# B products on GpSimd at the head of a tile, and the residual through an identity matmul, in a two-layer Mamba and MoE kernel

## What is computed

```python
def mamba_block(seq, ...):
    u, z = split(in_proj(seq)); u = silu(causal_conv4(u) + conv_b)
    dt, Bm, Cm = split(u @ x_proj_w.T)
    dt = softplus(dt @ dt_proj_w.T + dt_proj_b)
    def step(h, inputs):                      # 128 channels d, 16 states n
        dA = exp(dt_t[:, :, None] * A)
        h = dA * h + (dt_t * u_t)[:, :, None] * B_t[:, None, :]
        y = einsum('bdn,bn->bd', h, C_t)
    y = (ys + u * D) * silu(z)
    return y @ out_proj_w.T
...
x = x + mamba(ln(x));  t = tokens(x);  t = t + experts(ln(t))      # twice
```

## Time and profile before

| what | us |
|---|---|
| median of 3 runs | 1973.01 |
| lowest and highest run | 1966.05, 1973.41 |
| the profiled execution's own time | 1973.6 |
| its span | 1971.8 |
| PE busy | 1445.4 (73%) |
| DVE busy | 1359.6 (69%) |
| POOL busy | 1138.6 (58%) |
| ACT busy | 928.1 (47%) |

### The profile page before, as it was taken

One profiled execution on the slowest core, in us unless ns is written; L12 is line 12 of the kernel. 1 busy time (PEld: TensorE's weight loads), 2 busy tenths in 40 slices (PEclk: granted clock), 3 DMA queues, 4 the chain that ended last, 5 costly groups with the idle time before them and its releaser, 6 DMA issues. The chain is left out here.

```text
span 1971.8 us, 28551 instructions
## 1 busy us (share of the span) xinstructions
PE 1445.4 (73%) x7776; PEld 980.9 (50%) x7777; DVE 1359.6 (69%) x1913; ACT 928.1 (47%) x1695; POOL 1138.6 (58%) x788
## 2 busy tenths in 40 slices
PE   6666766667656599999956766666667662799993
PEld 4333333333314499999834333333333222799992
DVE  2899999999995422222143999999999967444443
ACT  6666677667743011111136666677666731011111
POOL 0687788888880244444302888888878850355540
PEclk9889898998968699999968788998998866899996
DMA  3655566555638110111034565566555634111114
GB/s 110 147 135 121 129 144 146 125 126 134 145 79 354 54 41 32 38 37 36 26 126 98 129 138 121 129 143 139 134 121 135 148 136 188 38 48 48 47 41 152
DMA packets 75964, 217.61 MB, mean 110 GB/s; under 512 B 11856, under 2 KB 27408, under 8 KB 72592
## 3 DMA queue, kind: packets, MB, share of 16 engines
q1 hardware_dynamic: 67664, 194.53, 38.9%
q0 software_dynamic: 8256, 22.56, 3.5%
HBM read 178.34 MB, written 38.70 MB: 110 GB/s over the span
## 5 line engine op out<-in xcount | busy, mean ns | idle before, releaser
L669 POOL TENSOR_TENSOR L_hc<-L_h,L_cbq 128x1536 f32<-128x1536 f32 x192 | 660.1, 3438 | 210.6 <-DVE L_h L587 207.5
L492 ACT ACTIVATE ps<-L_dwq,L_negA 128x384 f32<-128x384 f32 x768 | 426.7, 574 | 227.4 <-DVE L_h L587 215.5
L364 PE MATMUL ps<-L_hc,same 128*32 128x384 f32 x1536 | 190.0, 571 | 238.9 <-POOL L_hc L669 238.9
L574 DVE TENSOR_TENSOR L_dbu<-L_dwq,ps 128x768 f32<-128x768 f32 x288 | 270.7, 941 | 29.4 <-DVE L_carry L649 13.1
L587 DVE TENSOR_TENSOR_SCAN L_h<-ps,L_h,L_dbu 128x384 f32<-128x384 f32 x288 | 275.0, 1002 | 12.9 <-ACT ps L492 12.8
L587 DVE TENSOR_TENSOR_SCAN L_h<-ps,L_carry,L_dbu 128x384 f32<-128x384 f32 x288 | 274.2, 1001 | 6.5 <-DVE L_dbu L574 4.7
L364 PEld LDWEIGHTS ps<-L_hc,same 128*32 128x32 f32 x1536 | 31.5, 113 | 358.2 <-POOL L_hc L669 324.3
L1151 DVE COPY Xn<-L_w 128x2048 f32 x86 | 107.6, 1253 | 117.1 <-PE ps L1101 108.3
L1134 ACT ACTIVATE L0e_hT<-ps 128x512 f32<-128x512 f32 x86 | 51.3, 597 | 267.2 <-PE ps L1101 267.2
L678 POOL TENSOR_TENSOR L_dbp<-L_dwq,L_cbq 128x768 f32<-128x768 f32 x96 | 175.1, 1824 | 0.0
L323 PE MATMUL ps<-Xn,L_fold 128*128 (+1 forms) x480 | 103.3, 368 | 89.2 <-DVE L_dw L595 89.2
(11 more groups left out here) (278 smaller groups left out, 2301.4 us busy)
## 6 DMA issues: line engine op xcount, KB each, us to landing
L_dwq<-dw_rows SPq DMA_DIRECT2D x192, 384.0 KB, 6.2
L_cbq<-cb_rows SPq DMA_DIRECT2D x192, 240.0 KB, 9.9
dw_rows<-L_dw SPq DMA_DIRECT2D x48, 384.0 KB, 2.3
L_w<-in_up SPq DMA_DIRECT2D x16, 1024.0 KB, 11.7
L_w<-in_down SPq DMA_DIRECT2D x8, 1024.0 KB, 26.6
tok_rows<-Xn SPq DMA_DIRECT2D x6, 768.0 KB, 13.1
L0s_got<-results SPq DMA_DIRECT2D x18, 256.0 KB, 2.9
L1s_got<-results SPq DMA_DIRECT2D x18, 256.0 KB, 3.5
```

The lines of the kernel that those rows point to most:

```text
L364: mm = nc.tensor.matmul(y_ps[g * QW:(g + 1) * QW, :], same[:, 0:QW], hc[:, (k % 2) * Q + g, :], start=False, stop=(k == Q - 1))
L492: nc.scalar.activation(da(r, c), dwq[:, r, c % Q, 0, :], ACT.Exp, scale=negA[:, 0, c:c + 1]).then_inc(sem["da"], 1)
L574: nc.vector.tensor_tensor(dbu[:, at:at + 2, :], dwq[:, r, 2 * i:2 * i + 2, 1, :], spread(b_ps(r, k)), ALU.mult).then_inc(sem["dbu"], 1)
L669: nc.gpsimd.tensor_tensor(hc[:, at:at + Q, :], h[:, Q * k:Q * k + Q, :], cbq[:, r, k, :].unsqueeze(1).to_broadcast([P, Q, T]), ALU.mult).t ...
```

## The change

Four of the 16 B products of a tile were made by POOL, two behind C0 and two behind C1. Now six are: scans 10 and 11 take theirs from `times_b2` (two planes), scans 12 to 15 from `times_b3` (four planes in one instruction), and both stand ahead of C0 in POOL's order. DVE makes five products of two planes instead of six, and `dbu` has ten planes of its own instead of a ring of six. B of the third quarter is sent through DRAM with the rest, so that `cbq` and `bc` have six rows instead of five (each `cbq` load is 288 KB). The residual is no longer added by DVE: PE adds X to the output's PSUM bank by a matmul with the identity, and ACT copies the sum back to X behind decay 14 (`take_x`).

```diff
-QR = Q + 1
+QR = Q + 2
...
-        dbu = sb("dbu", [P, 6, T])
-        dbp = sb("dbp", [P, Q, T])
+        dbu = sb("dbu", [P, 10, T])
+        dbp = sb("dbp", [P, 6, T])
...
             def spread_b(t, r, k):
-                wait(pe, sem["dbu"], 6 * t + 2 * k - 2)
+                wait(pe, sem["dbu"], 5 * t + (-1, 0, 2)[k])
...
             def project_out(t):
                 pe.wait_ge(sem["yz"], t + 1)
+                x = X[:, :, bass.ds(t * PT, PT)].rearrange("p i (h w) -> p h i w", w=SIDE)
+                nc.tensor.matmul(zb_ps[:, 0:T // 2].rearrange("p (h i w) -> p h i w", i=2, w=SIDE), ident[:], x,
+                                 start=True, stop=False)
                 for j in range(2):
                     mm = nc.tensor.matmul(zb_ps[:, 0:T // 2], w_out[:, j, :], js(yz[:])[:, j, :],
-                                          start=(j == 0), stop=(j == 1))
+                                          start=False, stop=(j == 1))
...
+            def take_x(t):
+                act.wait_ge(sem["out"], t + 1)
+                x = X[:, :, bass.ds(t * PT, PT)].rearrange("p i (h w) -> p h i w", w=SIDE)
+                nc.scalar.copy(x, zb_ps[:, 0:T // 2].rearrange("p (h i w) -> p h i w", i=2, w=SIDE)).then_inc(sem["res"], 1)
...
+                    if c == 14 and not (isinstance(t, int) and t == 0):
+                        take_x(t - 1)
...
-                    if k < Q - 1:
+                    if 2 * k + i < 5:
                         times_b(t, r, p, k, i)
...
-                        if j == 6:
-                            residual(t - 1)
...
+            def times_b2(t, r, p):
+                pool.wait_ge(s_cb[r], 64 * (p + 1))
+                pool.wait_ge(s_dw[r], 64 * (p + 1))
+                wait(pool, sem["scan"], (t - 1) * N + 12)
+                nc.gpsimd.tensor_tensor(dbp[:, 0:2, :], dwq[:, r, 2:4, 1, :], spread(cbq[:, r, Q + 1, :]), ALU.mult
+                                        ).then_inc(sem["dbu_p"], 1)
+
+            def times_b3(t, r):
+                wait(pool, sem["scan"], t * N)
+                nc.gpsimd.tensor_tensor(dbp[:, 2:6, :], dwq[:, r, :, 1, :],
+                                        cbq[:, r, Q, :].unsqueeze(1).to_broadcast([P, Q, T]), ALU.mult
+                                        ).then_inc(sem["dbu_p"], 1)
...
             def tile(t, r, p, last):
+                times_b2(t, r, p)
+                times_b3(t, r)
                 for k in range(Q):
                     times_c(t, r, p, k)
-                    if k < 2:
-                        times_b(t, r, p, k)
                     if k == 2 and not last:
                         lost(t + 2)
```

More of the change, by code:

```diff
@@ L559, in _ @@
             tile_pairs(act, pair)
+            take_x(NT - 1)
         @block.vector
@@ L567, in times_b @@
                     dve.wait_ge(s_dw[r], 64 * (p + 1))
[L568 to L573, removed]
+                at = 4 * k + 2 * i
+                wait(dve, sem["scan"], (t - 1) * N + at + 2)
                 nc.vector.tensor_tensor(dbu[:, at:at + 2, :], dwq[:, r, 2 * i:2 * i + 2, 1, :], spread(b_ps(r, k)),
@@ L577, in scan @@
             def scan(t, c, slot):
-                k, g = c // Q, c % Q
+                k = c // Q
                 dve.wait_ge(sem["da"], t * N + c + 1)
-                if k < Q - 1:
-                    dve.wait_ge(sem["dbu"], 6 * t + c // 2 + 1)
+                if c < 10:
+                    dve.wait_ge(sem["dbu"], 5 * t + c // 2 + 1)
                 else:
-                    dve.wait_ge(sem["dbu_p"], 2 * t + g // 2 + 1)
+                    dve.wait_ge(sem["dbu_p"], 2 * t + (1 if c < 12 else 2))
                 wait(dve, sem["hc"], Q * (t - 1) + k + 1)
@@ L587, in scan @@
                 nc.vector.tensor_tensor_scan(h[:, c, :], da(t % 2 if isinstance(t, int) else int(slot is None), c),
-                                             dbu[:, c % 6, :] if k < Q - 1 else dbp[:, g, :], first, ALU.mult, ALU.add
+                                             dbu[:, c, :] if c < 10 else dbp[:, c - 10, :], first, ALU.mult, ALU.add
                                              ).then_inc(sem["scan"], 1)
@@ L602, in gate @@
                 nc.vector.tensor_tensor(yz[:], zs[:, r, :], y_ps, ALU.mult).then_inc(sem["yz"], 1)
[L604 to L608, removed]
             nc.vector.tensor_tensor(fold[:].rearrange("p g d -> p (g d)"), par("in_u"), par("taps"), ALU.mult
@@ L653, in _ @@
             gate(NT - 1, 1)
-            residual(NT - 1)
         @block.gpsimd
@@ L724, in send @@
                 bc_out, dt_out, w = count(t + 1), count(t + 1), count(t + 1)
-                decayed, driven, mixed, driven_p = count((t - 1) * N), count((t - 1) * 6), count((t - 1) * Q), count((t - 1) * 2)
+                decayed, driven, mixed, driven_p = count((t - 1) * N), count((t - 1) * 5), count((t - 1) * Q), count((t - 1) * 2)
                 sp_.wait_ge(sem["bc_out"], bc_out)
@@ L1370, in pack @@
     state = g("x_proj_w")[4:].reshape(2, Q, Q, P)
-    put("bc", np.concatenate([state[1].transpose(1, 0, 2), state[0, Q - 1][:, None]], 1).reshape(Q * QR, P).T)
+    put("bc", np.concatenate([state[1].transpose(1, 0, 2), state[0, Q - 1][:, None], state[0, Q - 2][:, None]], 1).reshape(Q * QR, P).T)
     put("brep", np.repeat(state[0].reshape(N, P), QW, 0).T)
```

## The result

The changed kernel takes 2027.57 us (median of 4, 2027.01 to 2044.25) against 1973.2 before: ratio 1.0305, 95% interval 1.0276 to 1.0335. It is slower by 3%. The profiled execution took 2027.01, with a span of 2025.0.

A forecast was written before the change was run, and what follows sets the result against it. It took the bound to be the loop from POOL's C3 through C0, PE, ACT and scans: 22.2 + 0.94 = 23.14 us a tile against 22.17, so 1973.6 + 46.6 + 4 = 2024, rounded to 2025; range 1976 to 2060.

The forecast's parts named there:

- No gain from DVE's B product ahead of scan 8: DVE before scan 8: ACT's decay 8 sets the scan, so removing the product is worth 0 to 0.26 us, taken as 0.
- The residual's 0.45 a tile: DVE behind scan 13: without the residual the next B product could begin at 321.33 instead of 321.78, worth 0.45 us.
- Its replacement hidden: Residual through PE (0.4 to 0.8 us more) and ACT's copy (0.45 us at most), covered by other waits: worth 0.
- a sign of being wrong: C3 to C3 above 22.2 for another reason: the two `cbq` users, `lost`, or `take_x` in front of decay 15.
- C0 at 8.5, the loop of 22.2: POOL's C0 starts 8.5 us after C3, 3.2 later; through y0, `project_dt`, Abs and scans, C3 to C3 takes 22.2.
- The loop against the undisturbed tile: C3 to C3 at full clock: 22.2 us against 21.60 and 22.55, mean 22.08, so +0.1 a tile.
- The clock, 0.94 a tile: PE's low clock moves to y0 in five tiles of eight, 1.5 us each: 0.94 a tile, ends 0 and 2.2.
- in more than half of the tiles: Sign of being right: PE's granted clock is low from y0 on in more than half of the tiles.
- The start of a layer, 4 us in both: B products before the first C0 of a layer cost 0 to 5.2 us, taken as 2 for each layer.
- The late `cbq`: Rival: the larger load lands late and delays POOL's chain, costing from 2.4 us of lateness on; 0.10 together with every tile paying.
- DVE's busy time: Sign of being right: DVE's busy time falls by 48 x 1.27 = 61 us and the span doesn't follow.
- the loop without the clock: Rival: POOL's loop holds but PE's clock adds nothing, 22.2 to 22.5 us a tile, 1979 to 1993; chance 0.20.

## Why the prediction was right

It said 2025 with 1976 to 2060, and 2027.57 was measured. The chain, the waits and the loop are as predicted. How the added time parts into loop and clock is not, and that the sum came within 3 us owes something to luck. One more row of the trace before is needed, the C3 that follows those of the earlier trace rows:

```profile
413.98 3.43 POOL L669 TENSOR_TENSOR L_hc<-L_h,L_cbq 128x1536 f32<-128x1536 f32 x1
```

Point by point:

- *No gain from DVE's B product ahead of scan 8.* Right. Scan 8 waits for ACT's decay 8 either way, and the wait grows by what the product took (28.7 against 3.8 us in a stage; 26.1 in 23 tiles is 1.13 each, and 1.15 was predicted). The totals agree twice (1963.75 against 1962.14; stages 1033.1 against 1033.8).
- *The residual's 0.45 a tile.* Too large as its price. It was read from a tile in which the residual itself was late; the typical tiles give 0.21 to 0.26. The loop of 22.2 doesn't suffer from it, since it starts from the same tile and takes the lateness away with the residual.
- *Its replacement hidden.* Right by itself: no loss with it alone. ACT's copy takes 0.30, the identity matmul 0.59 at the full clock. In the changed kernel it is not fully hidden, since the copy waits for `project_out` and decay 15 stands behind it; the prediction named this as a sign of being wrong and gave it no price. Its stages are 3.8 us longer with the replacement than without.
- *C0 at 8.5, the loop of 22.2.* Right: 8.57, and 22.23 and 22.11 when the clock is up. The Abs wait of 1.0 and 0.1 is 0.9 and 0.04 there. That this loop runs over `project_dt` behind y0 is shown by the move of `project_dt` and `project_bc` (1976.8).
- *The loop against the undisturbed tile.* Here the prediction had +0.1 us, against 22.08. Both tiles of the earlier trace rows were a little disturbed. The tile that follows them took 21.39 (392.59 to 413.98), and 21.39 and 22.42 are the usual lengths, with PE kept busy too (21.40 and 22.42). Their mean is 21.91, so the loop is 0.27 a tile longer. In the stages it is more: with PE kept busy in both kernels they are 1064.9 and 1044.5, a difference of 20.4 us or 0.43 a tile. Of it 9.8 us lie in the first four tiles of the two layers.
- *The clock, 0.94 a tile.* The sum set 22.2 + 0.94 against a mean of 22.17 that had the old kernel's clock losses in it. So it counted 0.03 a tile for the loop and 0.94 for the clock. The runs give 0.43 for the loop with the layers' starts and 0.65 for the clock (1.07 in the changed kernel less 0.43 in the one before). The two errors point opposite ways: 46.6 predicted for the stages, 51.5 measured. The picture behind the 0.94 was partly wrong as well. It was not five tiles of eight with two instructions slow. In the first layer it was every second tile, from the fourth on, with all three slow (Abs waits 2.96), in the second two tiles in all; so the sign "in more than half of the tiles" did not come true. The rest of the loss came where a low stretch on `u_in` holds up DVE's product. The prediction had named `u_in` only as a place where low stretches do no harm.
- *The start of a layer, 4 us in both.* The first tile, from scan 0 to scan 0, grew by 0.8 and 3.1 us.
- *The late `cbq`.* Didn't happen beyond the first tile.
- *DVE's busy time.* It fell by 49 us and not by 61. The 61 adds up lengths of instructions, and neighbours overlap: the product of 0.93 in the earlier trace rows held up the next scan by some 0.87.

The rival "the loop without the clock" gave 1979 to 1993. The changed kernel with PE kept busy runs at 1972.7, 6 us under that range. So that rival nearly describes this kernel once the clock is held up.

Open: the parts outside of the Mamba stages are 906 to 915 us in these runs, without an edit there, and I don't know why.

## What to carry to other kernels

An engine that is 96% busy need not be worth relieving: read at each place which wait would be next. Here DVE already waited 0.26 us for ACT. When work is moved ahead of an old instruction, follow that instruction's consumer and everything that is queued behind the consumer on its own engine; here the edit was on POOL and the harmful wait on DVE, by way of PE and ACT. And a wait of PE can cost twice, if it brings the low clock onto the path: keep PE's gaps off the critical queue, or fill all of them.

## What the runs showed of the hardware

- A late operand can cost more by the clock than by its lateness. In the changed kernel ACT's Abs waited 2.96 us for `project_dt` where PE ran at the low clock behind C0, and some 0.9 in the same place where PE ran at the full clock. Matmuls that compute nothing new, put into PE's gaps, took 51.5 us off the changed kernel's stages (granted clock 0.84 and 0.87 to 0.98) and 19 us off the whole kernel before. With one gap of three filled, the low stretches lay at another gap and the median stayed where it was (2025.14).
- The same code can settle in different patterns. In the changed kernel one layer alternates 22.7 and 25.1 us tiles (565.9 in all) and the other runs mostly at 22.5 to 23.4 (550.4), by where the low stretches fall.
- A change that takes 0.2 us a tile off the path (the residual) can give nothing in the end (ratio 1.000). DVE's waits for the spread behind `u_in` grew from 4.1 to 14.4 us in the first stage at the same time.
